# Both feed-forward fronts written as one: normalisation, router and shared feed-forward in one table-ordered program ahead of routing

## The chip, the cores and the metric

One Trainium2 core runs the whole kernel. The metric is the device time of one execution in microseconds, lower is better. A core has five instruction queues that matter here: PE (TensorE, matrix products), DVE (VectorE), ACT (ScalarE), POOL (GpSimd) and SP (SyncE, which only issues transfers). Each queue runs its own instructions in the order in which they are written; between queues there are only semaphores.

## The reference

The input is 4096 tokens of width 512. Three residual steps follow one another, and the change touches the first and the last.

```python
x = x + 0.5 * ffn(layernorm(x))        # first front and first expert stage
x = x + attention(layernorm(x))
x = x + 0.5 * ffn(layernorm(x))        # second front and second expert stage

def ffn(h):                            # E=32 experts, K=6, I=256, CAP=192
    logits = h @ gate_w.T
    scores = sqrt(softplus(logits))
    idx = top_k(scores + bias, K)                      # choice
    w = 1.5 * scores[idx] / sum(scores[idx])           # weights
    pos = running count of earlier choices of the same expert; valid = pos < CAP
    routed = sum over valid choices of w * down_e(silu(gate_e(h)) * up_e(h))
    shared = clip(silu(h @ sg.T) * (h @ su.T), -10, 10) @ sd.T
    return routed + shared
```

Products run on PE in fp32r after each operand has been split in a high part and a remainder (`hi`, `lo`), three products for one (`split_products`).

## The kernel before, in words

A feed-forward step has a front and an expert stage. The front must deliver `slots`, the table that says which token rows each expert gathers. The expert stage (`routed_experts`) then takes 32 experts in turn: POOL gathers 192 rows, PE computes, POOL adds the result to the output in memory.

The front works on G = 8 groups of 512 tokens. For a group, "norm and router" means: load `x`, statistics on DVE (L334), `h` on DVE (L347), 16 transposes on PE (L420), the high part on ACT (L295), the remainder on DVE (L354, L391), eight router products on PE (L428). "Shared work" of a group means gate and up (48 products of 512 columns) and down (24), with the silu on ACT, the product and the clip on DVE, the high part on ACT and the remainder.

Before, three programs stand one behind the other, each in a block of its own, so that all queues meet at its end. `setup` loads and splits constants and the shared weights. `dense_ffn` computes norm and router of all eight groups and the shared work of groups 0 to 4 (GA = 5): its loop body does the shared work of group g beside norm and router of group g+1, and groups 6 and 7 get norm and router alone behind the loop. In the first front POOL splits the attention weights there too (L282, L284). `route` computes the routing on DVE, with the shared work of groups 5 to 7 written between its steps (`inner`, L670 and L672; `add_residual`, L679), and remainders on POOL (L641). Its last part is the hot loop: for each of 32 tiles of 128 tokens DVE writes `hot_a` and `hot_b` (L777, L782), ACT scales `hot_a` by the tile number (L632), POOL scales it by the row number (L660), and PE adds eight small products to `r_ps_tab` (L874, L875).

Of the kernel before, what the change touches and what calls it, by code (L numbers as in the profile page):

```python
# [7 lines left out]
F32 = mybir.dt.float32  # L8
# [22 lines left out]
GA = 5  # L31
HT_OF = {5: 1, 6: 0, 7: 2}
# [32 lines left out]
NO_SLOT = 4000.0  # L65
SWIGLU_LIMIT = 10.0
# [22 lines left out]
def allocate_kept(nc, ctx):  # L89
    k = Kept()  # L90
    k.ffn_semaphores = []

    def sb(name, shape, dt):
        return ctx.enter_context(nc.sbuf_tensor(name, shape, dt))

    k.ident = sb("ident", [P, P], F32)
    k.causal_bf = sb("causal_bf", [P, P], BF16)
    k.ident_bf = sb("ident_bf", [P, P], BF16)
    k.upto_bf = sb("upto_bf", [P, P], BF16)
    k.ones_bf = sb("ones_bf", [P, P], BF16)  # L100
    k.ln_eps = sb("ln_eps", [P, 1], F32)
    k.rms_eps = sb("rms_eps", [P, 1], F32)
    k.shared_hi = sb("shared_hi", [P, WALL], F32R)
    k.shared_lo = sb("shared_lo", [P, WALL], F32R)
    k.router = sb("router", [P, KB, 3, E], F32R)
    k.wqkv_hi = sb("wqkv_hi", [P, KB, 6 * DH], F32R)
    k.wqkv_lo = sb("wqkv_lo", [P, KB, 6 * DH], F32R)
    k.wo_hi = sb("wo_hi", [P, H, D], F32R)
    k.wo_lo = sb("wo_lo", [P, H, D], F32R)
    return k  # L110


def setup(nc, a, k, htab, accs):

    with ExitStack() as ctx:
        sb = lambda name, shape, dt: ctx.enter_context(nc.sbuf_tensor(name, shape, dt))
        sem = lambda name: ctx.enter_context(nc.semaphore(name))
        raw_shared = sb("raw_shared", [P, WALL], F32)
        raw_router = sb("raw_router", [P, KB, E], F32)
        raw_causal = sb("raw_causal", [P, P], F32)  # L120
        raw_upto = sb("raw_upto", [P, P], F32)
        zeros = sb("zeros", [HALF, ROW], F32)
        no_weights = sb("no_weights", [P, KB, E], F32)
        zeroed, dumps, hi_ready = sem("setup_zeroed"), sem("setup_dumps"), sem("setup_hi")
        loaded = {name: sem(f"setup_loaded_{name}") for name in ("small", "shared", "shared_down")}
        with nc.Block() as block:

            @block.sync
            def _(sp):
                for name, dst, src in (("small", raw_router[:, :, :], a["router_w"]), ("small", k.ident[:, :], a["ident"]),  # L130
                                       ("small", raw_causal[:, :], a["causal"]), ("small", raw_upto[:, :], a["upto"]),
                                       ("shared", raw_shared[:, 0:WGU], a["w_shared"][:, 0:WGU]),
                                       ("shared_down", raw_shared[:, WGU:], a["w_shared"][:, WGU:])):
                    sp.dma_start(dst, src).then_inc(loaded[name], 16)

                sp.wait_ge(zeroed, 1)
                sp.dma_start(htab[DUMP:ROWS, :], zeros[:, :]).then_inc(dumps, 16)
                for acc in accs:
                    sp.dma_start(acc[DUMP:ROWS, :], zeros[:, 0:D]).then_inc(dumps, 16)
                sp.wait_ge(dumps, 16 * (1 + len(accs)))  # L140

            @block.gpsimd
            def _(pool):
                pool.memset(k.ones_bf[:, :], 1.0)
                pool.memset(no_weights[:, :, :], 0.0)
                pool.memset(k.ln_eps[:, :], LN_EPS)
                pool.memset(k.rms_eps[:, :], RMS_EPS)
                pool.memset(zeros[:, :], 0.0).then_inc(zeroed, 1)

            @block.scalar  # L150
            def _(act):
                act.wait_ge(zeroed, 1)
                act.activation(k.router[:, :, 2, :], no_weights[:, :, :], ACT.Copy)
                act.wait_ge(loaded["small"], 16 * 4)
                act.activation(k.router[:, :, 0, :], raw_router[:, :, :], ACT.Copy).then_inc(hi_ready, 1)
                act.activation(k.ident_bf[:, :], k.ident[:, :], ACT.Copy)
                act.activation(k.causal_bf[:, :], raw_causal[:, :], ACT.Copy)
                act.activation(k.upto_bf[:, :], raw_upto[:, :], ACT.Copy)
                act.wait_ge(loaded["shared"], 16)
                act.activation(k.shared_hi[:, 0:WGU], raw_shared[:, 0:WGU], ACT.Copy).then_inc(hi_ready, 1)  # L160
                act.wait_ge(loaded["shared_down"], 16)
                act.activation(k.shared_hi[:, WGU:], raw_shared[:, WGU:], ACT.Copy).then_inc(hi_ready, 1)

            @block.vector
            def _(dve):
                for n, (lo, raw, hi) in enumerate(((k.router[:, :, 1, :], raw_router[:, :, :], k.router[:, :, 0, :]),
                                                   (k.shared_lo[:, 0:WGU], raw_shared[:, 0:WGU], k.shared_hi[:, 0:WGU]),
                                                   (k.shared_lo[:, WGU:], raw_shared[:, WGU:], k.shared_hi[:, WGU:]))):
                    dve.wait_ge(hi_ready, n + 1)
                    dve.tensor_tensor(lo, raw, hi.bitcast(F32), ALU.subtract)  # L170


def dense_ffn(nc, a, k, n, src, acc, htab, logits, ht_hi, ht_lo):

    with ExitStack() as ctx:
# [10 lines left out]
        silu = [sb(f"d_silu{b}_", [P, GTOK], F32) for b in range(FB)]  # L189
        inter = [sb(f"d_inter{b}_", [P, GTOK], F32) for b in range(FB)]  # L190
        in_hi = [sb(f"d_in_hi{u}_", [P, FB, GTOK], F32R) for u in range(2)]
        in_lo = [sb(f"d_in_lo{u}_", [P, FB, GTOK], F32R) for u in range(2)]
        ps_t = [pb(f"d_ps_t{i}_") for i in range(2)]
        ps_gate = [pb(f"d_ps_gate{b}_") for b in range(FB)]
        ps_up = [pb(f"d_ps_up{b}_") for b in range(FB)]
        ps_down = [pb(f"d_ps_down{i}_") for i in range(2)]
        lg_t = sb("d_lg_t", [3 * E, GTOK], F32)

        d_bank = (ps_down[0], ps_down[1], ps_gate[0], ps_up[0])

        t_bank = lambda c, late: ps_gate[c - 2] if late and c >= 2 else ps_t[c % 2]
        lg_banks = lambda late: ps_up if late else ps_t
        x_loaded = [[sem(f"d_x_loaded{u}{m}_") for m in range(2)] for u in range(3)]
        h_stored = [sem(f"d_h_stored{u}_") for u in range(2)]
        y_stored = [sem(f"d_y_stored{u}_") for u in range(2)]
        stats_ready, std_ready, h_ready = sem("d_stats_ready"), sem("d_std_ready"), sem("d_h_ready")
# [1615 lines left out]
```

## Time and profile before

| | us |
|---|---|
| median of 3 runs | 1814.66 |
| lowest, highest | 1813.36, 1817.22 |
| the profiled execution's own time | 1805.24 |
| its span in the trace | 1803.5 |
| first front: slots written at | 281.3 |
| second front: first transposes, slots written | 1223.0, 1479.6 |

Times of the trace count from its first instruction. The profiled execution is 9.4 us below the median of the timed runs. PE is busy 85% of the span, DVE 65%, ACT 55%, POOL 43%; such shares are averages over stages with different limits, so the stages are read one by one. The granted PE clock is 1.00 at 2.4 GHz and 0.50 at 1.2 GHz.

### The profile page before, as it was taken

How to read it: one execution, taken by the hardware profiler on the slowest of the kernel's cores; microseconds unless marked ns; L12 is line 12 of the kernel's file. 1: busy time of each engine (PE TensorE's matmuls, PEld its weight loads, DVE VectorE, ACT ScalarE, POOL GpSimd, SP SyncE). 2: the span in 40 equal slices, each digit the busy share in tenths (PEclk: the TensorE clock that was granted, in tenths of full speed). 3: DMA queues.
4: the chain of work that ended last, by engine and by line, in shares of the span. 5: the costliest groups of instructions: out<-in, count | busy, mean ns of one | idle time of the engine just before them, and what ended most of it. 6: DMA issues, size and time to landing. Idle time of an engine off the chain costs nothing. (4 is left out here: it accounts for less than half of the span.)

```text
span 1803.5 us, 27507 instructions
## 1 busy us (share of the span) xinstructions
PE 1524.5 (85%) x8626; PEld 1256.3 (70%) x8628; DVE 1167.5 (65%) x2369; ACT 991.7 (55%) x2038; POOL 777.4 (43%) x677
## 2 busy tenths in 40 slices
PE   4997766999998289999999999878986759999994
PEld 3775555877777267887887887656765548787773
DVE  5666676777776156666666665645676577777773
ACT  3334144777776156666666666533333146777773
POOL 3000163556554376556557655310000263656653
PEclk9998887999999689999999999998997888999998
DMA  6444314999996211111111111014444316899994
GB/s 214 150 146 165 117 35 140 264 259 264 264 264 174 66 42 41 48 36 59 42 42 59 36 42 41 25 62 141 154 146 141 108 39 211 260 261 262 264 265 85
DMA packets 87196, 244.98 MB, mean 136 GB/s; under 512 B 17649, under 2 KB 18609, under 8 KB 78673
## 3 DMA queue, kind: packets, MB, share of 16 engines
q1 hardware_dynamic: 64592, 192.12, 31.2%
q0 software_dynamic: 22528, 51.92, 13.7%
q8 instruction: 40, 0.66, 0.1%
q14 instruction: 36, 0.29, 0.0%
HBM read 175.25 MB, written 68.76 MB: 135 GB/s over the span
## 5 line engine op out<-in xcount | busy, mean ns | idle before, releaser
L1077 DVE TENSOR_TENSOR e_w_lo<-e_raw,e_w_hi 128x1024 fp32r<-128x1024 f32 x192 | 233.9, 1219 | 109.8 <-ACT e_w_hi L1001 91.7
L1001 ACT ACTIVATE e_w_hi<-e_raw 128x1024 fp32r<-128x1024 f32 x192 | 202.5, 1056 | 29.6 <-PEq L570 17.0
L1582 POOL TENSOR_SCALAR t_prob<-t_prob,t_inv 128x128 f32<-128x128 f32 (+7 forms) x128 | 111.8, 873 | 221.0 <-DVE t_inv L1489 221.0
L1156 PE MATMUL e_ps_gate<-e_xt,e_w_hi 128*128 128x384 f32 x512 | 164.7, 384 | 28.8 <-DVE e_w_lo L1077 28.6
L953 POOL DMA_INDIRECT e_xg<-htab,e_gather_idx x128 | 138.5, 1082 | 63.1 <-issue 42.8
L1156 PE MATMUL e_ps_up<-e_xt,e_w_hi 128*128 128x384 f32 x512 | 151.9, 361 | 0.0
L964 POOL DMA_INDIRECT x_after_ffn<-e_y,e_add_idx x64 | 102.4, 1600 | 110.6 <-DMA x_after_ffn<-e_y,e_add_idx 87.9
L964 POOL DMA_INDIRECT out<-e_y,e_add_idx x64 | 102.3, 1598 | 110.4 <-DMA out<-e_y,e_add_idx 88.2
L1384 ACT ACTIVATE t_prob<-a_wide,t_neg_max,a_q_scale 128x128 f32<-128x128 f32 (+7 forms) x128 | 106.4, 831 | 53.3 <-DVE t_neg_max L1483 53.1
L1157 PE MATMUL e_ps_gate<-e_xt,e_w_lo 128*128 128x192 f32 x512 | 132.9, 260 | 0.0
L1157 PE MATMUL e_ps_up<-e_xt,e_w_lo 128*128 128x192 f32 x512 | 129.4, 253 | 0.0
L637 POOL MEMSET r_no_slots<- 128x96 bf16 x2 | 0.4, 180 | 295.8 <-POOLq L228 295.8
L1156 PEld LDWEIGHTS e_ps_gate<-e_xt,e_w_hi 128*128 128x128 f32 x512 | 101.0, 197 | 38.5 <-issue 21.9
L1494 DVE TENSOR_TENSOR t_pt<-a_bank,t_pt 128x512 fp32r<-128x512 f32 x144 | 96.3, 684 | 42.7 <-ACT t_pt L1391 41.9
L1391 ACT ACTIVATE t_pt<-a_bank 128x512 fp32r<-128x512 f32 x144 | 84.0, 596 | 69.2 <-PE a_bank L1659 68.9
L74 PE MATMUL e_ps_down<-e_w_hi,e_in_hi 128*96 128x512 f32 x256 | 101.1, 395 | 2.9 <-ACT e_y L1033 2.9
L1157 PEld LDWEIGHTS e_ps_gate<-e_xt,e_w_lo 128*128 128x128 f32 x512 | 102.4, 200 | 0.0
L76 PE MATMUL e_ps_down<-e_w_hi,e_in_lo 128*96 128x512 f32 x256 | 101.4, 396 | 0.0
L75 PE MATMUL e_ps_down<-e_w_lo,e_in_hi 128*96 128x512 f32 x256 | 100.2, 392 | 0.0
L1157 PEld LDWEIGHTS e_ps_up<-e_xt,e_w_lo 128*128 128x128 f32 x512 | 98.0, 191 | 0.0
L1481 DVE TENSOR_REDUCE t_top<-a_wide 128x1 f32<-128x128 f32 (+7 forms) x128 | 95.7, 748 | 1.6 <-PE a_wide L1651 1.6
L1156 PEld LDWEIGHTS e_ps_up<-e_xt,e_w_hi 128*128 128x128 f32 x512 | 96.5, 189 | 0.0
(318 smaller groups left out, 4644.7 us busy)
## 6 DMA issues: line engine op xcount, KB each, us to landing
e_raw<-in_w_experts SPq DMA_DIRECT2D x64, 1536.0 KB
htab<-d_h SPq DMA_DIRECT2D x16, 1024.0 KB, 4.2
d_x<-in_x SPq DMA_DIRECT2D x16, 512.0 KB, 5.0
q_x<-x_after_ffn SPq DMA_DIRECT2D x32, 256.0 KB, 3.2
t_res<-x_after_ffn SPq DMA_DIRECT2D x32, 256.0 KB, 2.6
x_after_attention<-t_res SPq DMA_DIRECT2D x32, 256.0 KB, 2.0
d_x<-x_after_attention SPq DMA_DIRECT2D x16, 512.0 KB, 5.4
x_after_ffn<-d_y SPq DMA_DIRECT2D x5, 1024.0 KB, 7.4
```

What stands on the lines that cost most here:

```text
L74: pe.matmul(out, wh, mh, start=first, stop=False)
L75: pe.matmul(out, wh, ml, start=False, stop=False)
L76: return pe.matmul(out, wl, mh, start=False, stop=last)
L953: pool.indirect_dma_start(xg[u][q][:, :], None, htab, bass.IndirectOffsetOnAxis(ap=gather_idx[u][:, q:q + 1], axis=0)).then_inc(gathered[u ...
L964: pool.indirect_dma_start(acc, bass.IndirectOffsetOnAxis(ap=add_idx[u][:, q:q + 1], axis=0), y[u][q][:, :], None, compute_op=ALU.add).then ...
L1001: act.activation(w_hi[u][:, cols], raw[u][:, cols], ACT.Copy).then_inc(hi_ready, 1)
L1077: dve.tensor_tensor(w_lo[u][:, cols], raw[u][:, cols], w_hi[u][:, cols].bitcast(F32), ALU.subtract).then_inc(lo_ready, 1)
L1156: pe.matmul(out, w[0][:, c, cols], xt[u][:, c, :, :], start=c == 0, stop=False)
L1157: got = pe.matmul(out[:, 0:CAP], w[1][:, c, cols], xt[u][:, c, 0, :], start=False, stop=c == KB - 1)
L1384: act.activation(prob[:, u, 0:width(i)], ps_s[i % 2][:, 0:width(i)], ACT.Exp, scale=q_scale[:, i // H % QSLOTS, i % H:i % H + 1], bias=neg ...
L1494: dve.tensor_tensor(pt[1][g % 3][:, :], bank("prob", T, c)[:, :], pt[0][g % 3][:, :].bitcast(F32), ALU.subtract).then_inc(p_lo, 1)
L1582: pool.tensor_scalar(prob[:, u, 0:width(i)], prob[:, u, 0:width(i)], inv[:, u:u + 1], 1.0, ALU.mult, ALU.mult).then_inc(p_ready, 1)
```

## The change

`setup`, `dense_ffn` and `route` become one function, `front`, in one block.

- Norm and router of the eight groups are the frame of every queue's program. `h` is now written by ACT (Identity with a scale and a shift), and the operands of six groups are kept (PLACES = 6) where there were three.
- The shared work is cut into 48 pieces (`piece`: gate, up or half of down, 12 products each). Tables (`PE_AT`, `DVE_AT`, ...) say behind which numbered spot of a queue's frame a piece is written. Up to spot 24 of PE (in group 6, behind its first two transposed chunks) there are 12 pieces, two to a group on the whole; at spot 24 there are 22; six are at each of 25 and 29; the last two at 30 and 31. No piece stands behind the start of routing.
- The clip and the remainder of all groups are on POOL; the hot loop has no POOL work and no tile-number product: ACT does the row number (L471), PE adds four products a tile, and the tile number comes from counts that DVE takes behind the loop (L664 to L672).
- The two halves of the logits are folded by PE with a constant matrix, where DVE added them.
- The residual input of the shared work is loaded again, a tile at a time (`xs`, six buffers), for all eight groups; it was loaded again for three.
- Constants and shared weights are loaded and split within the first front. The attention weights are loaded and split in the first expert stage: ten chunks of 128x512, one for each of experts 4 to 13, between a gather and a scatter on POOL.

```diff
-GA = 5
-HT_OF = {5: 1, 6: 0, 7: 2}
+PLACES = 6
+XS = 6
+PE_AT = (2, 4, 4, 4, 5, 5, 8, 9, 12, 13, 16, 17, 20, 21, 24, 24, 24, 24, 24, 24, 24, 24, 24, 24, 24, 24, 24, 24, 24,
+    24, 24, 24, 24, 24, 24, 24, 25, 25, 25, 25, 25, 25, 29, 29, 29, 29, 29, 29, 29, 29, 30, 30, 30, 31)
...
+        def at_spots(table, dense):
+            count = [0]
+
+            def spot():
+                for p in range(6 * G + 6):
+                    if table[p] == count[0] and piece(p)[0]:
+                        dense(*piece(p))
+                count[0] += 1
+            return spot
...
+                def dense(kind, g, b):
+                    if kind == "up":
+                        i = FB * g + b
+                        pool.wait_ge(mul_done, i + 1)
+                        pool.tensor_scalar(inter[i % 2][:, :], inter[i % 2][:, :], SWIGLU_LIMIT, -SWIGLU_LIMIT,
+                                           ALU.min, ALU.max).then_inc(clipped, 1)
+                        pool.wait_ge(ihi_ready, i + 1)
+                        pool.tensor_tensor(in_lo[g % 2][:, b, :], inter[i % 2][:, :], in_hi[g % 2][:, b, :].bitcast(F32),
+                                           ALU.subtract).then_inc(ilo_ready, 1)
...
+                for g in range(G):
+                    turn(g, 0)
+                    turn(g, 1)
+                    spot()
+                    if g:
+                        fold_logits(g - 1)
+                        spot()
+                    turn(g, 2)
+                    turn(g, 3)
+                    spot()
+                    router(g)
+                    spot()
+                fold_logits(G - 1)
+                spot()
...
+                for e in range(4, 4 + chunks):
+                    gather_next(e // 2, e % 2)
+                    split_chunk(e - 4)
+                    scatter(e // 2 - 1, e % 2)
```

What the program of a queue is at three places.

First, VectorE in the middle of the first front's routing, around the mask (L724 before, L599 after). Before:

```order
L714 SCALAR_TENSOR_TENSOR r_t_0<-r_seg,r_t_0 128x1024
L679 SCALAR_TENSOR_TENSOR r_xs_0<-r_ps_down,r_xs_0 128x512
L679 SCALAR_TENSOR_TENSOR r_xs_0<-r_ps_tab,r_xs_0 128x512
L718 TENSOR_TENSOR r_t_0<-r_t_0,r_per_tok 128x1024
L679 SCALAR_TENSOR_TENSOR r_xs_0<-r_ps_down,r_xs_0 128x512
L721 SCALAR_TENSOR_TENSOR r_t_0<-r_t_0 128x1024
L679 SCALAR_TENSOR_TENSOR r_xs_0<-r_ps_tab,r_xs_0 128x512
L724 TENSOR_TENSOR r_mask<-r_t_0 128x1024
L670 TENSOR_TENSOR r_inter<-r_silu,r_ps_up 128x512
L672 TENSOR_SCALAR r_inter<-r_inter 128x512
```

and after:

```order
L590 SCALAR_TENSOR_TENSOR r_t_0_74<-r_seg,r_t_0_73 128x1024
L593 TENSOR_TENSOR r_t_0_75<-r_t_0_74,r_per_tok 128x1024
L596 SCALAR_TENSOR_TENSOR r_t_0_74<-r_t_0_75,r_t_0_73 128x1024
L599 TENSOR_TENSOR r_mask_79<-r_t_0_74,r_t_0_72 128x1024
L606 COPY r_t_0_72<-d_ps_lg 128x32x16
L606 COPY r_t_0_72<-d_ps_fold 128x32x16
```

The residuals and the product of shared work (L679, L670) have gone from between the steps; the routing steps stand directly behind one another.

Second, ScalarE in group 6 of the first front, after the change (L399 is the high part of a transposed chunk, L413 the silu, L418 the high part of a shared product, L387 the normalisation of the next group):

```order
L379 ACT_TABLE_LOAD
L379 ACTIVATE d_std_0<-d_mv_0,ln_eps 128x4
L399 ACTIVATE ht_hi_0_59<-d_ps_t_0 128x512 x2
L418 ACTIVATE d_in_hi_0<-d_inter_0 128x512
L413 ACT_TABLE_LOAD
L413 ACTIVATE d_silu_0<-d_ps_gate 128x512
L418 ACTIVATE d_in_hi_0<-d_inter_0 128x512
L413 ACTIVATE d_silu_0<-d_ps_gate 128x512
...
L399 ACTIVATE ht_hi_0_59<-d_ps_t_0 128x512 x2
L387 ACTIVATE d_h_0_70<-d_x_0_68,d_shift_0,d_rstd_0 128x512 x4
```

The pair of L413 and L418 repeats through group 5 before the last two chunks of group 6 (L399) are taken, so the shared work of groups 2 to 5 stands ahead of the routers of groups 6 and 7; before, groups 6 and 7 had their routers behind group 4.

Third, GpSimd in the first expert stage, before:

```order
L973 COPY e_gather_idx_0<-slots 96x2 x2
L953 DMA e_xg_0<-htab,e_gather_idx_0 96x544 x10
L964 DMA x_after_ffn<-e_y_0,e_add_idx_0 4192x512 x2
L953 DMA e_xg_0<-htab,e_gather_idx_0 96x544 x2
L964 DMA x_after_ffn<-e_y_0,e_add_idx_0 4192x512 x2
```

and after:

```order
L898 DMA e_xg_0<-htab,e_gather_idx_0 96x544 x10
L909 DMA x_after_ffn<-e_y_0,e_add_idx_0 4192x512 x2
L898 DMA e_xg_0<-htab,e_gather_idx_0 96x544 x2
L909 DMA x_after_ffn<-e_y_0,e_add_idx_0 4192x512 x2
L898 DMA e_xg_0<-htab,e_gather_idx_0 96x544 x2
L915 CAST wqkv_hi<-d_xs_0 128x512
L917 TENSOR_TENSOR wqkv_lo<-d_xs_0,wqkv_hi 128x512
```

A cast (L915) and a subtraction (L917) of one chunk of attention weights now stand between a gather (L898) and a scatter (L909).

## Rows read from the trace of the kernel before

**Rows 1.** The page: span.
```profile
span 1803.5 us, 27507 instructions
```

**Rows 2.** Busy time by stretch, with PE clock, DMA share and GB/s.
```profile
core 0: us, PE busy (x) PEld busy (x) DVE busy (x) ACT busy (x) POOL busy (x), PEclk, DMA share, GB/s
...
52.00:74.00 22.00, 21.45 (x104) 16.81 (x103) 14.13 (x29) 8.09 (x12) 0.00 (x0) 1.00 0.43 144
142.00:166.30 24.30, 13.30 (x65) 9.47 (x63) 15.72 (x38) 7.66 (x14) 0.00 (x0) 0.78 0.35 130
166.30:281.30 115.00, 81.76 (x489) 63.92 (x490) 82.54 (x165) 38.60 (x55) 40.18 (x41) 0.87 0.28 92
1223.00:1362.10 139.10, 124.11 (x584) 96.82 (x584) 87.68 (x181) 50.49 (x78) 0.00 (x0) 0.96 0.42 144
1362.10:1479.60 117.50, 83.18 (x489) 65.13 (x490) 82.84 (x165) 38.50 (x55) 40.61 (x41) 0.87 0.27 90
340.00:400.00 60.00, 54.97 (x344) 47.23 (x342) 44.90 (x81) 44.34 (x80) 35.43 (x26) 1.00 0.90 260
```

**Rows 3.** Timeline, first front: issue of x, h, transposes, first router product.
```profile
14.56 1.97 SPq L233 DMA_DIRECT2D d_x<-in_x  x4
...
22.02 1.92 DVE L347 TENSOR_SCALAR d_h<-d_x,d_mv,d_rstd 128x512 f32<-128x512 f32 x4
...
23.99 1.97 PE L420 MATMUL d_ps_t<-ident,d_h 128*128 128x128 f32 x8 [23.99 <-DVE d_h L347]
...
29.89 0.74 PE L428 MATMUL d_ps_t<-ht_hi,router 128*96 128x512 f32 x1 [1.41 <-DVE ht_lo L354]
```

**Rows 4.** Timeline, PE: first and last of 24 gate and up products; transposes.
```profile
197.27 0.40 PE L74 MATMUL r_ps_gate<-ht_hi,shared_hi 128*128 128x512 f32 x1
...
202.64 0.40 PE L76 MATMUL r_ps_up<-ht_hi,shared_lo 128*128 128x512 f32 x1
...
148.03 1.94 PE L420 MATMUL d_ps_t<-ident,d_h 128*128 128x128 f32 x8 [3.80 <-DVE logits L359]
...
156.07 1.09 PE L420 MATMUL d_ps_t<-ident,d_h 128*128 128x128 f32 x8
```

**Rows 5.** Waits in the first routing, 166.3 to 281.3 us: total, times, longest.
```profile
DVE r_inter L670 <- ACT r_silu L612: 10.2, 2, 6.6
...
PE r_ps_gate L74 <- POOL r_in_lo L641: 6.9, 1, 6.9
...
DVE r_hot_a L777 <- PE r_ps_tab L875: 6.8, 1, 6.8
...
DVE r_t L685 <- ACT r_t L605: 3.5, 1, 3.5
```

**Rows 6.** Groups by line, VectorE, same stretch: count | busy, mean ns.
```profile
L670 DVE TENSOR_TENSOR r_inter<-r_silu,r_ps_up 128x512 f32<-128x512 f32 x4 | 2.7, 684 | 10.2 <-ACT r_silu L612 10.2
L679 DVE SCALAR_TENSOR_TENSOR r_xs<-r_ps_tab,r_xs 128x512 f32<-128x512 f32 x4 | 2.7, 684 | 0.5 <-PE r_ps_tab L76 0.5
```

**Rows 7.** Timeline, VectorE: two tiles of the hot loop.
```profile
248.10 0.42 DVE L782 TENSOR_TENSOR r_hot_b<-r_slot_b,r_iota_b 128x512 bf16<-128x512 bf16 x1
...
248.71 0.42 DVE L782 TENSOR_TENSOR r_hot_b<-r_slot_b,r_iota_b 128x512 bf16<-128x512 bf16 x1
```

**Rows 8.** Groups by line: scaling a hot tile on GpSimd and ScalarE.
```profile
L660 POOL TENSOR_SCALAR r_part_a<-r_hot_a,r_part_id 128x384 bf16<-128x384 bf16 x64 | 56.7, 903 | 13.3 <-DVE r_hot_a L777 12.9
...
L632 ACT ACTIVATE r_tile_a<-r_hot_a,r_tile_id 128x384 bf16<-128x384 bf16 x64 | 39.3, 615 | 32.7 <-DVE r_hot_a L777 32.7
```

**Rows 9.** Timeline: VectorE's normalise beside GpSimd's split.
```profile
33.36 3.48 POOL L284 TENSOR_TENSOR wqkv_lo<-d_y,wqkv_hi 128x1536 fp32r<-128x1536 f32 x1
...
36.16 6.68 DVE L347 TENSOR_SCALAR d_h<-d_x,d_mv,d_rstd 128x512 f32<-128x512 f32 x4
```

**Rows 10.** Waits in the first expert stage, 300 to 560 us.
```profile
POOL x_after_ffn L964 <- DMA x_after_ffn<-e_y,e_add_idx: 74.9, 26, 4.3
...
PE e_ps_gate L1156 <- DVE e_w_lo L1077: 14.1, 23, 0.8
```

More of the change, by code:

```diff
@@ L105, in allocate_kept @@
     k.router = sb("router", [P, KB, 3, E], F32R)
[L106 to L109, printed above, removed]
-    return k
[L113 to L170, printed above, removed]
@@ new lines, in allocate_kept, with piece, place_of_group, staged_buffers @@
+    return k
+def piece(p):
+    g, r = divmod(p, 6)
+    kind = ("gate", "up", "down")[r % 3]
+    there = g > 0 if kind == "down" else g < G
+    return (kind, g - 1 if kind == "down" else g, r // 3) if there else (None, g, 0)
+def place_of_group(g):
+    return g % PLACES
+def staged_buffers(nc, places, name, u, n):
+    part = KB * GTOK * 4
+    at = (nc.sbuf_base + 31) // 32 * 32
+    places.enter_context(nc.sbuf_tensor(f"{name}{u}_{n}", [P, 2 * KB * GTOK], F32))
+    hi = nc.alloc_sbuf_tensor_at(f"ht_hi{u}_{n}", [P, KB, GTOK], F32R, offset=at)
+    lo = nc.alloc_sbuf_tensor_at(f"ht_lo{u}_{n}", [P, KB, GTOK], F32R, offset=at + part)
+    return at, hi, lo
@@ L178, in dense_ffn, with front @@
+def front(nc, a, k, n, src, acc, accs, htab, slots, staged, raw, xs, w_loaded, y_stored):
     with ExitStack() as ctx:
@@ L201, in dense_ffn @@
[L201 to L206, printed above, removed]
-        t_ready, t_hi, t_lo = sem("d_t_ready"), sem("d_t_hi"), sem("d_t_lo")
@@ L604, in _ @@
+                act.wait_ge(lg_taken, G)
+                for u in range(2):
+                    act.wait_ge(h_stored[u], 16 * (G // 2))
+                act.activation(t2[:, :, :], logits[:, :, :], ACT.Abs)
                 act.drain()
@@ new lines, in router @@
+                def router(g):
+                    pe.wait_ge(t_lo, 4 * g + 4)
+                    if g:
+                        pe.wait_ge(lg_out, g)
+                    elif n == 0:
+                        pe.wait_ge(setup_lo, 1)
+                    at = place_of_group(g)
+                    for c in range(KB):
+                        for part, ht in enumerate((ht_hi, ht_lo)):
+                            got = pe.matmul(ps_lg[0:3 * E, :], k.router[:, c, :, :].rearrange("p s e -> p (s e)"),
+                                            ht[at][:, c, :], start=(c == 0 and part == 0),
+                                            stop=(c == KB - 1 and part == 1))
+                    got.then_inc(lg_ready, 1)
```

1028 lines of the change are left out of this document (495 added, 533 removed).

## The prediction

> **What bounds the kernel now.** I read the windows first, stage by stage, because the change leaves attention alone and touches the expert stages only by ten small pieces of work. The span is 1803.5 us [rows 1]; the two fronts end at 281.3 and 1479.6. A front has two halves. Up to the last logits PE is the bound: a loop body of 22.0 us holds 21.45 us of PE work at clock 1.00, with ACT busy 8.09 and DVE 14.13 [rows 2]. Behind the loop the last two groups get norm and router alone, and 24.3 us pass with PE busy 13.3 and its clock at 0.78 [rows 2]. The second half, the routing, takes 115.0 and 117.5 us, and there VectorE's chain is the bound (busy 82.5), because the queue holds shared work too and waits for it: 10.2 us in two waits for a silu, 6.8 for the hot tables while PE finishes the last down products, themselves 6.9 late on a remainder of GpSimd [rows 2, 5].
>
> So time between first transposes and slots is 281.3 - 24.0 = 257.3 and 1479.6 - 1223.0 = 256.6 us [rows 2, 3].
>
> **The change, part by part.** I rebuild both halves of a front; T is the first transposes, L the last logits.
>
> *T to L.* All shared work is now here, so this half gets longer. Twelve products of a piece cost half of 24; the first and the last of 24 start 5.37 us apart over 23 steps, so 0.2335 each and 2.80 a piece [rows 4]. 47 of the 48 pieces stand ahead of the last logits: 131.7. Sixteen pairs of transposed chunks at 0.95 (8 transposes last 1.09, and the next start before that end) [rows 4]: 15.2. Eight routers of eight products, 0.2335 each: 14.9. Eight folds, smaller than a pair of chunks, 0.5 each: 4.0. Together 165.8 of PE work. What PE cannot cover: the first group's chain from transposes to router, 5.9 us with 1.9 of work in it [rows 3], so 4; the last two chunks of groups 6 and 7, which have no piece between them and the gate that needs them, 1.8 each; the last logits' way through VectorE, 0.5. That is 173.9. For stalls that I cannot see I add 3: 177. Bounds: 0 and, by the rival below, some 20.
>
> Why should PE run through? In the interleaved groups 1 to 5 it has 2 pieces, 4 chunks, router and fold, 9.8 us. ScalarE has four more instructions a group than in the old body (h). At 0.6 each (a scaling of 384 columns takes 0.615 [rows 8]) that is 8.09 + 2.4 = 10.5 in the old body, but a group now has about half of the old body's silus and splits, so near 9.0 of 9.8. That is close. VectorE loses h and clip and gets 7 to 8. Followed queue by queue, each chunk's high part and remainder end under the piece that stands behind it, with about 1 us to spare; where ScalarE changes its table for silu and for square root, the margin is smallest. GpSimd's clip and remainder: 3.48 us for 1536 columns and 0.903 for 384 are both 2.3 ns a column [rows 8, 9], so 1.2 each for 512; product, clip, high part and remainder take about 4, and two or three pieces (5.6 to 8.4) stand between an up and the down that needs it. Hidden. If the cover were gone (one piece, 2.8), it would cost 1.2 for each of eight groups. Loads: five more groups' inputs, 5 MB a front, at a DMA share of 0.42 and 0.28 [rows 2]; hidden. On SP a tile's store waits for its residual ahead of the store of the last h; that h is read by nobody until routing.
>
> *T itself.* In the first front x was issued at 14.56 and transposed at 23.99, 9.4 later [rows 3], behind the setup block. Now x is issued third in SP's queue, near 1.7. With 9.4 plus a little for h on ScalarE (4 at about 0.55 against 1.92 for four [rows 3]) T comes at 11.5. But gate of group 0 waits for the shared weights behind 3.8 MB of transfers, split by near 23 us, about 3.5 later than PE would be there. So L = 11.5 + 177 + 3.5 = 192. The second front keeps T = 1223.5 and gives L = 1400.5, where it was 1362.1.
>
> *L to slots.* From 115: VectorE is busy 82.5. Shared work leaves it: six products and twelve residuals at 0.684 [rows 6] and six clips at some 0.4, 14.7. The hot loop: with GpSimd running a tile takes 0.90 (its own instruction, 0.903), at a moment without it 0.61, two hot tables apart [rows 7, 8]; ScalarE's scaling takes 0.615, so 0.62 is the new pace and 28 tiles give 8.0 back. Adding the logits' halves and small steps: 1.8. New: tile numbers, two passes over 1024 columns and two reductions, up to 1.2 each, 4.5 (bounds 2.5 and 6). Busy 62.5. Waits that stay: exponent 3.5 [rows 5], square root with its table 2.5, the counting products 2, last products and transposes 2.2, drains 2.5: 12.7. Sum 75 (bounds 70 and 82).
>
> Slots: 192 + 75 = 267, 14.3 earlier; 1400.5 + 75 = 1475.5, 4.1 earlier. Fronts: -18.4.
>
> *Expert stage of the first step.* Ten chunks on GpSimd, 1.2 for the subtraction and about 0.6 for the cast. GpSimd waits there for the landing of the last addition, 74.9 us in 26 waits, 2.9 each [rows 10], and the chunk stands ahead of just that wait: hidden. Their 2.6 MB come at a DMA share of 0.90 and 260 GB/s [rows 2]: 10 us if nothing is free; six of ten are issued at the stage's start, when the weights of experts 0 and 1 are there and those of expert 2 are not yet asked for, so 4 chunks, 1 MB, 4 us at full price, less half for the tenth that is free. 2 us. And VectorE beside GpSimd: four normalisations of h took 6.68 beside a split and 1.92 alone, 4.8 more for 3.5 of GpSimd's work [rows 3, 9]. PE waits for the weights' remainder of VectorE already, 23 times, 0.6 each [rows 10], so a delay there reaches it. I take 0.2 a chunk, 2 us; bounds 0 and, if VectorE loses all the 1.8 us of a chunk and PE all of VectorE's, 18. Stage: +4.
>
> The Trainium skill (SBUF — State Buffer, "Who interferes with whom") says that a VectorE instruction with two inputs in SBUF contends with a GpSimd instruction that reads SBUF, and that whoever is first holds the port for its whole instruction. The weights' remainder is such an instruction, and the trace bears the rule out in kind [rows 9]; by it a chunk can cost the whole 1.8 us, ten of them 18, which is the third rival below.
>
> **Sum.** -14.3 - 4.1 + 4 = -14.4. Against the profiled execution's span, 1803.5 gives 1789.1; against the median of the runs, which lies 9.4 above that execution's time, 1814.7 gives 1800. A measurement tells this kernel from itself to about 0.2%, 3.6 us.
>
> **Rivals.**
> Margins hold better (faster still): no stalls where I allow 3 a front and nothing in the expert stage: -14.4 - 6 - 4 = -24, 1790. For it: the old loop ran at 21.45 of 22.0. Against: the new interleaving is tighter.
> The interleaved groups run at the pace of their chain, not of PE (slower). The two late groups show that chain bare: 24.3 us for two, 12.2 each [rows 2]. If half of a piece more stands uncovered, 13.5 against my 9.8, for five groups in two fronts: +37, less the 6 allowed: 1800 + 31 = 1831. The transposes after a wait of 3.80 us took 1.94 against 1.09 [rows 4], the lower of PE's two clock levels, so such gaps also slow what follows. It decides from 11.9 us a group, where 6 + 14.4 are eaten. Against it: pieces stand where those groups had nothing.
> GpSimd's splits block VectorE in the expert stage: +18 for +4, so -0.4: 1814, no change. Against it: GpSimd there mostly issues gathers and has 2.9 of slack.
> That nothing is gained because the hidden work comes back is half true already: 16.8 us of shared work for each of three groups leaves a routing that covered it, and L moves 26 to 38 later. That is in the sum.
>
> **Numbers.** Forecast 0.48 (own range 1793 to 1808), faster still 0.20, chain pace 0.22, blocking 0.10. The predicted time is 1800. From 1783 to 1819 takes in the first, second and fourth and the mild end of the third. Faster 0.68, same 0.11 (blocking, and the middle of the chain's case), slower 0.21.
>
> **What would show it.** T near 11.5; last logits near 192 and 1400; routing near 75 with VectorE hardly waiting; hot pace 0.62; PE busy over 0.93 of T to L at clock 1.00; an expert pace near 9.0 us also for experts 4 to 13. The prediction is wrong if interleaved groups take 12 us or more, if the hot loop stays at 0.9 (then something other than GpSimd slowed it, +9 a front), or if the first expert stage grows by more than 10.

## The result: 2.25% slower, and the profile after

The changed kernel takes 1855.42 us (median of 4 runs, 1853.50 to 1858.60), the kernel before 1814.45 (4 runs, 1813.36 to 1817.22): ratio 1.0225, 95% interval 1.0207 to 1.0244. I had said 1800, between 1783 and 1819. So 41 us are lost where 14 were to be won.

First the page of the profiled execution, its span and the slices that the loss stands in (40 equal ones, a digit is a tenth).

```profile
span 1853.1 us, 26194 instructions
...
PE   6999448767799648999999999996999547999985
...
DMA  7735117765899621111101111115646105999994
```

The span is 49.6 longer [rows 1]. From the seventh to the eleventh slice, the first expert stage, PE stands at 6 to 8 tenths and DMA falls to 5; in the second expert stage, at the right end, nothing of the kind is seen. Busy time by stretch says the same, and it says how the fronts did:

```profile
15.00:199.60 184.60, 177.17 (x821) 142.22 (x822) 75.89 (x150) 77.49 (x123) 30.50 (x32) 0.98 0.58 190
199.60:273.40 73.80, 26.24 (x157) 18.95 (x157) 63.51 (x146) 27.44 (x39) 4.08 (x2) 0.55 0.08 19
273.00:400.00 127.00, 93.61 (x517) 83.52 (x516) 73.56 (x128) 70.17 (x119) 66.47 (x51) 0.83 0.70 203
400.00:500.00 100.00, 70.55 (x387) 62.42 (x388) 49.61 (x87) 52.41 (x91) 54.84 (x39) 0.88 0.63 172
500.00:600.00 100.00, 90.70 (x576) 79.10 (x575) 72.84 (x131) 70.95 (x129) 60.19 (x46) 1.00 0.92 259
1276.30:1300.00 23.70, 21.63 (x98) 17.16 (x99) 11.07 (x25) 14.44 (x25) 1.89 (x2) 0.80 0.69 244
1276.30:1456.70 180.40, 173.86 (x821) 140.26 (x822) 72.38 (x148) 74.28 (x118) 30.52 (x32) 0.96 0.56 189
1456.70:1530.10 73.40, 26.27 (x157) 18.96 (x157) 63.47 (x146) 27.44 (x39) 4.08 (x2) 0.54 0.08 19
```

The first row is T to L of the first front, the second its routing; the last two are those of the second front. PE is busy 177.2 of 184.6 us, and routing takes 73.8 and 73.4 where it took 115.0 and 117.5 [rows 2]. But from 400 to 500 PE is busy 70.6 of 100 and the DMA share is 0.63; it was 0.90 with PE at 0.92 in a stretch of that stage before [rows 2].

I cut the span of each execution at six moments: slots of the first front written (S1), first and last of the experts' scaled outputs in that stage (`e_y`), first maximum of attention, first transposes of the second front (T2), its slots (S2). Worked out from the traces by the starts of these instructions, one trace a kernel, in us:

```
kernel               S1    to first  all of its  to attention  to T2   to S2   to end   span
                           output    rounds
before              281.0    30.4      274.2        63.7       573.7   256.3   324.2   1803.5
changed             273.2    31.7      333.6        63.0       574.8   253.6   323.2   1853.1
semaphore           274.5    34.1      281.5        65.2       574.8   253.8   323.4   1807.3
before, bare drain  285.6    31.6      356.2        64.3       574.1   259.0   325.8   1896.6
doubled remainder   271.9    34.2      301.0        64.6       576.3   253.9   323.3   1825.2
hot on GpSimd       282.7    34.4      283.7        64.9       576.4   263.2   323.2   1828.5
half chunks         271.4    30.7      281.6        65.2       575.2   255.0   325.9   1805.0
wait for landing    271.9    34.6      334.3        65.0       574.7   254.9   323.5   1858.9
late loads          273.4    30.4      282.5        64.4       574.8   253.7   324.0   1803.2
chunk first         271.8    34.3      316.7        63.7       574.9   253.8   325.9   1841.1
double loads        269.7    30.2      282.8        65.2       573.9   254.8   324.0   1800.6
eighth loads        273.7    28.9      281.2        64.1       574.7   255.2   323.3   1801.1
loads in routing    271.5    29.0      281.9        64.5       573.4   253.7   324.6   1798.6
half splits         273.8    29.0      278.0        63.8       575.0   255.1   323.5   1798.2
```

Of the 49.6, the rounds of the first expert stage hold 59.4 (333.6 for 274.2); both fronts together win 10.5. All of the loss is in one stage. What waits there:

```profile
PE e_ps_t L1100 <- DMA e_xg<-htab,e_gather_idx: 67.1, 17, 10.5
...
POOL x_after_ffn L909 <- DMA x_after_ffn<-e_y,e_add_idx: 48.3, 14, 5.9
...
POOL wqkv_lo L917 <- issue: 30.8, 6, 6.6
...
POOL wo_lo L917 <- issue: 19.2, 4, 5.3
```

PE waits 67.1 us for gathered tokens (273 to 600 us); before, the same wait was 17.6 in all (281 to 600 us). GpSimd, which issues the gathers, stands still 50 us in 10 waits ahead of a chunk's remainder, and no releaser is named ("issue"). Its timeline shows one round of an expert (start, length, line, instruction, idle time before it):

```profile
349.53 1.48 POOL L898 DMA_INDIRECT e_xg<-htab,e_gather_idx  x1 [0.30 <-issue]
...
353.33 0.62 POOL L915 CAST wqkv_hi<-d_xs 128x512 fp32r<-128x512 f32 x1
359.01 1.26 POOL L917 TENSOR_TENSOR wqkv_lo<-d_xs,wqkv_hi 128x512 fp32r<-128x512 f32 x1 [5.07 <-issue]
360.44 1.48 POOL L909 DMA_INDIRECT x_after_ffn<-e_y,e_add_idx  x1 [0.17 <-issue]
...
364.52 1.47 POOL L898 DMA_INDIRECT e_xg<-htab,e_gather_idx  x1 [0.30 <-issue]
```

Two gathers, the chunk's high part (0.62), 5.07 us of nothing, its remainder (1.26), two additions; the next gathers come 15.0 after the last. PE's row of the same moment names the event at which the gap ends, the landing of the gathers (DMA e_xg):

```profile
358.85 1.54 PE L1100 MATMUL e_ps_t<-ident,e_xg 96*128 96x96 f32 x8 [3.69 <-DMA e_xg<-htab,e_gather_idx]
```

The gathers have landed by 358.85, and GpSimd's remainder starts at 359.01. One round earlier it is 343.95 and 344.12. The trace has the landing events themselves: in nine of the ten rounds the remainder starts 0.30 us after the last of the round's gathers has landed, in the first 0.89. Between the high part and the remainder the new code has a drain (`pool.drain()`), written there so that the remainder starts only when the high part is complete, and that is the suspect.

### The profile page after: what moved, and what is told of

It is laid out like the page before. It is cut to its first block and busy times, and to the rows that moved or that the text cites. A ratio compares the mean times of both kernels' runs of the same rounds, so it can differ in the third digit from the quotient of the medians.

```text
span 1853.1 us, 26194 instructions
## 1 busy us (share of the span) xinstructions
PE 1530.9 (83%) x8434; PEld 1272.3 (69%) x8436; DVE 1099.7 (59%) x2274; ACT 1029.0 (56%) x2096; POOL 780.2 (42%) x679
## 3 DMA queue, kind: packets, MB, share of 16 engines
q0 software_dynamic: 22528, 51.92, 13.6%
## 5 line engine op out<-in xcount | busy, mean ns | idle before, releaser
L1111 PE MATMUL e_ps_gate<-e_xt,e_w_hi 128*128 128x384 f32 x512 | 178.7, 408 | 21.4 <-DVE e_w_lo L1032 20.5
L898 POOL DMA_INDIRECT e_xg<-htab,e_gather_idx x128 | 145.3, 1135 | 66.0 <-issue 39.0
L909 POOL DMA_INDIRECT out<-e_y,e_add_idx x64 | 103.3, 1614 | 109.1 <-DMA out<-e_y,e_add_idx 87.2
L909 POOL DMA_INDIRECT x_after_ffn<-e_y,e_add_idx x64 | 104.1, 1627 | 87.8 <-DMA x_after_ffn<-e_y,e_add_idx 65.2
L1112 PE MATMUL e_ps_gate<-e_xt,e_w_lo 128*128 128x192 f32 x512 | 139.2, 272 | 0.0
L353 POOL TENSOR_SCALAR d_inter<-d_inter 128x512 f32<-128x512 f32 x32 | 19.6, 614 | 277.5 <-DVE d_inter L518 277.5
L1100 PE MATMUL e_ps_t<-ident,e_xg 96*128 96x96 f32 x512 | 61.6, 269 | 84.6 <-DMA e_xg<-htab,e_gather_idx 83.8
L1111 PEld LDWEIGHTS e_ps_gate<-e_xt,e_w_hi 128*128 128x128 f32 x512 | 109.4, 214 | 28.3 <-issue 17.5
L1100 PEld LDWEIGHTS e_ps_t<-ident,e_xg 96*128 96x128 f32 x512 | 52.9, 154 | 102.5 <-issue 78.4
L1112 PEld LDWEIGHTS e_ps_gate<-e_xt,e_w_lo 128*128 128x128 f32 x512 | 110.7, 216 | 0.0
```

Source lines behind the costliest of these rows:

```text
L898: pool.indirect_dma_start(xg[u][q][:, :], None, htab, bass.IndirectOffsetOnAxis(ap=gather_idx[u][:, q:q + 1], axis=0)).then_inc(gathered[u ...
L909: pool.indirect_dma_start(acc, bass.IndirectOffsetOnAxis(ap=add_idx[u][:, q:q + 1], axis=0), y[u][q][:, :], None, compute_op=ALU.add).then ...
L1100: got = pe.transpose(ps_t[c][:, at:at + HALF], xg[u][q][:, (2 * c + b) * P:(2 * c + b + 1) * P], k.ident[0:HALF, 0:HALF])
L1111: pe.matmul(out, w[0][:, c, cols], xt[u][:, c, :, :], start=c == 0, stop=False)
L1112: got = pe.matmul(out[:, 0:CAP], w[1][:, c, cols], xt[u][:, c, 0, :], start=False, stop=c == KB - 1)
```

## The experiments

Theory D: a drain on GpSimd waits for the gathers that it issued just before. Rivals: P, VectorE holds the remainder back by the shared port; L, the chunks' loads take the transfers' time. The kernels of one batch share their runs of the kernel before (medians 1819.4, 1817.4 and 1816.7 us in the three batches), so kernels of different batches are compared by their ratios.

**1. A semaphore for the drain.**

```diff
-                    pool.tensor_copy(hi, xs[c % XS][:, :])
-                    pool.drain()
+                    pool.tensor_copy(hi, xs[c % XS][:, :]).then_inc(att_hi, 1)
+                    pool.wait_ge(att_hi, c + 1)
```

> The changed kernel, in which GpSimd waits on a semaphore of its own high-part instruction where it drained between the high part and the remainder of a chunk. Theory D (the drain also waits until the gathers that GpSimd issued just ahead of it have landed, 4.1 to 6.6 us a chunk, and so stretches ten experts from 9.1 to 14.6 us): the gap between the two instructions falls below 0.5 us, the pace returns to about 9.1 to 9.3, and the time falls by 50 to 60, to 1795 to 1806. Rival P (the remainder is held back by VectorE's instructions on the same memory): the gap and the time stay, 1850 or more. Rival L (the chunks' loads steal from the weights' and the gathers' transfers): the gap goes or stays, but the pace remains above 12 us, 1835 or more.

1808.50 us, ratio 0.9948 (0.9929 to 0.9967): one line turns 2.25% slower into 0.5% faster. P and L fall as causes of the gap: the remainder is still there, still beside VectorE, and so are the loads. One round, on GpSimd:

```profile
360.96 2.35 POOL L910 DMA_INDIRECT x_after_ffn<-e_y,e_add_idx  x1 [0.16 <-DVE e_gather_idx L1046]
363.61 1.44 POOL L910 DMA_INDIRECT x_after_ffn<-e_y,e_add_idx  x1 [0.30 <-issue]
365.35 1.30 POOL L899 DMA_INDIRECT e_xg<-htab,e_gather_idx  x1 [0.30 <-issue]
366.96 0.96 POOL L899 DMA_INDIRECT e_xg<-htab,e_gather_idx  x1 [0.31 <-issue]
367.91 1.54 POOL L916 CAST wqkv_hi<-d_xs 128x512 fp32r<-128x512 f32 x1
369.54 1.29 POOL L918 TENSOR_TENSOR wqkv_lo<-d_xs,wqkv_hi 128x512 fp32r<-128x512 f32 x1
```

The gap is 0.1. Seven of the ten rounds last 10.0, not the 9.1 that I expected: more of that in 3, 5, 9 and 10.

**2. The drain alone, in the kernel before.** After the gathers of experts 4 to 13 of the first stage:

```diff
+                for e in range(4, 4 + alone):
+                    gather_next(e // 2, e % 2)
+                    pool.drain()
+                    scatter(e // 2 - 1, e % 2)
```

> The kernel before, with nothing added but a bare drain of GpSimd behind the gathers of experts 4 to 13 of the first expert stage; no chunks, the old fronts. Theory D: GpSimd's round for an expert becomes two gather issues, the wait for their landing and two addition issues, 14.6 less the 2.2 of a chunk's two instructions, so 12.4 against 9.1: +33, 1840 to 1855. Rivals P and L: nothing is there for the drain to wait for, 1815 as before.

1900.40 us, ratio 1.0456 (1.0428 to 1.0483). Ten bare drains cost twice what the change lost. In kind D is right and the rivals are out: there is no chunk here. In size I was wrong. Two rounds, the first from among the ten, the second from behind them:

```profile
369.92 1.47 POOL L964 DMA_INDIRECT x_after_ffn<-e_y,e_add_idx  x1 [5.37 <-issue]
...
374.43 1.47 POOL L953 DMA_INDIRECT e_xg<-htab,e_gather_idx  x1 [0.30 <-issue]
...
383.19 1.47 POOL L964 DMA_INDIRECT x_after_ffn<-e_y,e_add_idx  x1 [5.70 <-issue]
...
499.02 2.43 POOL L964 DMA_INDIRECT x_after_ffn<-e_y,e_add_idx  x1 [0.30 <-issue]
501.76 1.46 POOL L953 DMA_INDIRECT e_xg<-htab,e_gather_idx  x1 [0.30 <-issue]
...
509.51 1.47 POOL L964 DMA_INDIRECT x_after_ffn<-e_y,e_add_idx  x1 [5.04 <-DMA x_after_ffn<-e_y,e_add_idx]
```

The ten take 13.2 each where I worked out 12.4; in nine of them the addition starts 1.17 us after the gathers' landing. But the rounds behind them, with no drain, stay at 11.8 until the last experts, where the kernel before has about 9.1: now GpSimd waits 4 to 5 us for the landing of additions, and PE for gathers that were issued late. In the changed kernel the rounds fell back to about 9.1 soon after the last chunk. Why a late round stays late here isn't settled; no further run was made for it.

**3. The remainder twice.**

```diff
-                    pool.tensor_tensor(lo, ..., ALU.subtract).then_inc(att_split, 1)
+                    pool.tensor_tensor(lo, ..., ALU.subtract).then_inc(att_hi, 1)
+                    pool.wait_ge(att_hi, 2 * c + 2)
+                    pool.tensor_tensor(lo, ..., ALU.subtract).then_inc(att_split, 1)
```

> The changed kernel with the semaphore, and the remainder of each of the ten chunks computed twice in a row (1.27 us more of GpSimd a chunk, same output). If GpSimd's wait for the last additions (2.9 us a round before) hides a chunk: within 2 us of the kernel with the semaphore. If GpSimd's instruction blocks VectorE's remainders for its length and PE waits for it, as the third rival of the prediction has it: +13.

1828.58 us, ratio 1.0056 (1.0033 to 1.0079), 1.1% over the first run. The rounds are 19.5 longer, 1.95 for each of ten. Neither theory had that: the added instruction takes longer than the 1.27 it takes alone. One round:

```profile
349.28 2.22 POOL L918 TENSOR_TENSOR wqkv_lo<-d_xs,wqkv_hi 128x512 fp32r<-128x512 f32 x1
351.58 2.13 POOL L920 TENSOR_TENSOR wqkv_lo<-d_xs,wqkv_hi 128x512 fp32r<-128x512 f32 x1
```

Here both last over 2.1, where 1.28 is the bare length; the twenty of the ten rounds take 33.3 in all, the ten of experiment 1 12.9. PE's largest wait in these rounds (319 to 436 us) is for the gathers:

```profile
PE e_ps_t L1103 <- DMA e_xg<-htab,e_gather_idx: 18.4, 6, 4.3
```

What follows: with a second remainder GpSimd has no slack left, waits for nothing in eight of the ten rounds, and issues the gathers late.

**4. The hot tables scaled on GpSimd again.**

```diff
-                    act.activation(part_a[t % HOTS][...], hot_a[t % HOTS][...], ACT.Copy, scale=part_id[:, :])
+                    pool.tensor_scalar(part_a[t % HOTS][...], hot_a[t % HOTS][...], part_id[:, :], 1.0,
+                                       ALU.mult, ALU.mult)
```

> The changed kernel with the semaphore, and the scaling of the hot tables put back on GpSimd. If GpSimd's part of the hot loop set the pace of 0.90 a tile, by its own 0.903 or by holding VectorE: pace 0.9 for 0.62, 28 tiles, +8 a front, +16 in all. If the pace came from something else that the change removed: no difference.

1826.02 us, ratio 1.0039 (1.0020 to 1.0058), so 17.5 over the first run for 16 expected. First VectorE in the changed kernel, then here, then GpSimd here:

```profile
249.41 0.41 DVE L651 TENSOR_TENSOR r_hot_b<-r_slot_b,r_iota_b 128x512 bf16<-128x512 bf16 x1
...
250.01 0.41 DVE L651 TENSOR_TENSOR r_hot_b<-r_slot_b,r_iota_b 128x512 bf16<-128x512 bf16 x1
```

```profile
255.83 0.72 DVE L653 TENSOR_TENSOR r_hot_b<-r_slot_b,r_iota_b 128x512 bf16<-128x512 bf16 x1
...
256.73 0.72 DVE L653 TENSOR_TENSOR r_hot_b<-r_slot_b,r_iota_b 128x512 bf16<-128x512 bf16 x1
...
253.53 9.10 POOL L375 TENSOR_SCALAR r_part_a<-r_hot_a,r_part_id 128x384 bf16<-128x384 bf16 x10
```

A tile takes 0.60 and here 0.91, the same as GpSimd's 9.10 for ten; hot_b itself grows from 0.41 to 0.72. The first front's slots come 8.2 later, and the second front from T to its slots is 9.4 longer. So GpSimd's part did set the pace of the old hot loop. The Trainium skill (SBUF — State Buffer, "Who interferes with whom") says that VectorE and GpSimd share a pair of ports and that whoever holds it shuts the other out; 0.72 for 0.41 on VectorE here, and 2.2 for 1.28 on GpSimd in experiment 3, agree with it in kind.

**5 and 6. Half chunks; waiting for the landing itself.** The fifth cuts the ten chunks into twenty of 256 columns. The sixth keeps the semaphore and adds the very wait that the drain is thought to be:

```diff
                     pool.wait_ge(att_hi, c + 1)
+                    pool.wait_ge(gathered[e % 2], 32 * (e // 2 + 2))
```

> The kernel with the semaphore, its ten chunks of 512 columns cut into twenty of 256, one for each of experts 4 to 23. With ten chunks GpSimd waits only 0.16 us in most rounds of 10.0 us, so it sets the pace there and 0.9 us of each round comes on top of 9.1. If a round costs only what exceeds the slack (2.9 us before), a half chunk of about 1.5 us with its overhead fits: pace 9.1 to 9.4, 5 to 9 us faster than with whole chunks. If every chunk costs its share whatever its size, because it holds VectorE or the memory: twenty halves cost as much as ten wholes, no difference.

> The kernel with the semaphore, and between a chunk's high part and its remainder one more wait, on the semaphore of the two gathers just issued, so until they have landed; no drain. If the drain costs what it costs because it lasts until the gathers have landed, this has the changed kernel's pace of 14.6 and its time, +41 to +52 against the semaphore alone. If the drain has a cost of its own (a queue emptied, a restart), this is at least 15 us faster than the changed kernel.

Half chunks: 1805.74 us, 0.9931 (0.9910 to 0.9951); the interval overlaps that of the first run. Its rounds take 281.6 in all, those of the ten whole chunks 281.5: as the second theory has it, a chunk costs its share whatever its size. But the cost has changed its place: from 325 to 500 us PE waits 5.0 for VectorE's remainder of the weights, where it is 19.8 with whole chunks, and 13.6 for gathers, where it is 1.6.

Waiting for the landing: 1856.49 us, 1.0215 (1.0171 to 1.0259), the changed kernel's 1.0225 again, and its rounds take 334.3 against 333.6. GpSimd:

```profile
384.19 0.87 POOL L916 CAST wqkv_hi<-d_xs 128x512 fp32r<-128x512 f32 x1
390.64 1.27 POOL L919 TENSOR_TENSOR wqkv_lo<-d_xs,wqkv_hi 128x512 fp32r<-128x512 f32 x1 [5.59 <-DMA e_xg<-htab,e_gather_idx]
```

The gap of 5.59 is now put down to the gathers' landing by name. A semaphore on the landing and the drain cost the same, as far as the runs tell: the drain has next to no cost of its own beside it. By the landing events the remainder starts 0.15 after the landing here, and 0.30 with the drain.

**7. Late loads.** No chunk is loaded ahead of the first gathers; each is loaded two rounds before its use.

> The kernel with the semaphore, its chunks' loads issued two rounds before their use, so none ahead of the first gathers. With six loads there, the first gathered tokens reach TensorE 10.2 us after the slots, 8.0 before, and the first addition comes 38.1 after the slots, 34.0 before. If the six loads (1.5 MB, 6 us of transfer) delay the gathers: 2 to 4 us faster. If the delay is the table load for silu (1.28 us) and the clock: no difference.

1805.04 us, 0.9939 (0.9915 to 0.9964). By the runs alone that is not told from the first kernel; by the trace the place is clear. The first gathered tokens reach PE, with six loads ahead and with none:

```profile
284.60 1.54 PE L1101 MATMUL e_ps_t<-ident,e_xg 96*128 96x96 f32 x8 [10.17 <-DMA e_xg<-htab,e_gather_idx]
```

```profile
280.78 1.54 PE L1100 MATMUL e_ps_t<-ident,e_xg 96*128 96x96 f32 x8 [7.43 <-DMA e_xg<-htab,e_gather_idx]
```

10.1 and 7.4 us after the slots (274.5 and 273.4), and the first output comes after 30.4 instead of 34.1. By this pair of traces the six loads cost 3.7. Four other traces with six whole loads have 34.2 to 34.6, but that of the changed kernel, with the same loads, has 31.7, and why isn't known. The rounds are 282.5, hardly changed.

**8. The chunk ahead of the gathers.** The changed kernel with its drain; the additions are under way when it drains.

```diff
-                    gather_next(e // 2, e % 2)
                     split_chunk(e - 4)
+                    gather_next(e // 2, e % 2)
```

> The changed kernel with its drain, each chunk ahead of the round's gathers instead of behind them, so that at the drain the additions of the round before are under way, not gathers. If the drain waits for every transfer that GpSimd has issued: it lasts until those additions have landed, some 5 us, and the pace is 12.5 to 14.5, +35 or more against the semaphore. If it waits for gathers alone: the pace is about 10 and the time that of the semaphore.

1844.24 us, 1.0165 (1.0124 to 1.0205), some 39 over the semaphore. The ten gaps are 5.2, 2.1, 2.5, 1.4, 1.4, 7.1, 5.9, 6.9, 5.7 and 5.4. One of the short and one of the long:

```profile
374.02 1.59 POOL L917 TENSOR_TENSOR wqkv_lo<-d_xs,wqkv_hi 128x512 fp32r<-128x512 f32 x1 [1.36 <-DVE e_gather_idx L1045]
...
382.65 1.11 POOL L915 CAST wqkv_hi<-d_xs 128x512 fp32r<-128x512 f32 x1
390.87 1.47 POOL L917 TENSOR_TENSOR wqkv_lo<-d_xs,wqkv_hi 128x512 fp32r<-128x512 f32 x1 [7.11 <-issue]
```

The drain is not tied to gathers alone: by the landing events the remainder starts 0.30 after the last addition has landed in nine of the ten rounds, and 0.81 in the first. That also explains the short gaps. In those four rounds the second addition lands 4.2 to 4.5 us after its start, in the six others 7.1 to 9.7, and the drain ends with it each time. Why the landing is quick in some rounds and slow in others isn't known.

**9 and 10. What sets the 10.0?** Two theories are left for the rounds with a chunk: M, transfers; G, GpSimd's own work. The ninth loads each chunk twice, the tenth only 64 of its 512 columns (the kernel then leaves out seven eighths of attention's weights; GpSimd's arithmetic is whole).

> The kernel with the semaphore and late loads, each chunk's 256 KB loaded a second time into a buffer that is free (same arithmetic, same output). Theory M (the expert stage is bound by transfers: 264 GB/s at a DMA share of 0.92 before, so 0.26 MB more is 1.0 us more in a round, 9.0 to 10.0, and twenty halves cost what ten wholes cost): rounds with a chunk go from 10.0 to 11.0, +8 to +10. Theory G (GpSimd is full in these rounds, so its 1.9 us for a chunk set the pace): no difference.

> The kernel with the semaphore and late loads, of each chunk only 64 of 512 columns are loaded (the rest is what the buffer held, so attention has wrong weights); GpSimd's arithmetic stays whole. Theory M: rounds of 9.1 to 9.3 in place of 10.0, 6 to 8 us faster than with whole loads. Theory G: rounds of 10.0, no difference. If both limits lie at 10.0, this shows no gain and the halved arithmetic of the fourth run does.

1804.37 us (0.9933, 0.9910 to 0.9956) and 1804.20 us (0.9928, 0.9901 to 0.9954), rounds 282.8 and 281.2 where one whole load a chunk gave 282.5: an eighth of the bytes and twice the bytes make no difference. Busy time of the two, 330 to 400 us:

```profile
330.00:400.00 70.00, 60.22 (x354) 51.67 (x353) 53.83 (x85) 46.23 (x85) 60.11 (x43) 0.95 0.97 290
```

```profile
330.00:400.00 70.00, 62.02 (x369) 54.68 (x369) 53.59 (x85) 47.23 (x88) 60.35 (x42) 0.94 0.89 247
```

The DMA share is 0.97 and 290 GB/s in one, 0.89 and 247 in the other, at one pace. M falls: more was moved in the same time. GpSimd's full round in experiment 1 adds up without it: additions 2.35 and 1.44, gathers 1.30 and 0.96, chunk 1.54 and 1.29, gaps 0.16 + 0.30 x 3 + 0.08: 10.0.

That GpSimd doesn't wait is not yet that PE waits for GpSimd, and there is a theory that I left out here, though it is the third rival of the prediction: V, a chunk on GpSimd holds VectorE, and PE waits for VectorE. Two rows of VectorE in experiment 1, the second of them in the kernel before, and PE's only wait in the ten rounds of experiment 1 (321 to 421 us):

```profile
377.49 1.55 DVE L1033 TENSOR_TENSOR e_w_lo<-e_raw,e_w_hi 128x1024 fp32r<-128x1024 f32 x1 [1.63 <-ACT e_w_hi L959]
...
380.01 0.89 DVE L1046 COPY e_gather_idx<-slots 96x2 uint32 x1
```

```profile
378.64 0.16 DVE L1090 COPY e_gather_idx<-slots 96x2 uint32 x1
```

```profile
PE e_ps_gate L1112 <- DVE e_w_lo L1033: 13.8, 9, 1.8
```

A remainder of the weights that takes 1.22 before takes 1.55 beside the chunk's high part, and a copy of 0.16 takes 0.89 and ends where the chunk's remainder ends (380.87): 1.06 a round. PE waits up to 1.8 a round for VectorE, and for no gather; in the same ten rounds before (324 to 416 us) it waits 4.5 for VectorE and 2.0 for gathers. Over the stage VectorE's instructions last 9.5 longer in all, each taken against its median before, and the rounds are 7.3 longer. So by the traces whole chunks cost their time as V has it, and the doubled remainder of experiment 3 as G has it. No run separates the two: the bytes of 9 and 10 leave GpSimd's and VectorE's rows alike.

**11 and 12. A version for use.** The first six chunks are loaded in the first routing (DMA share 0.08, second row of the windows above), four late; the twelfth also cuts each chunk's arithmetic into halves.

> The kernel with the semaphore, the first six chunks loaded during the first routing, where the DMA share is 0.08, the other four late in the expert stage. Theory M: six rounds without extra traffic, 4 to 6 us faster than with late loads alone. Theory G: rounds with a chunk stay at 10.0, 0 to 1 us faster.

> The same, with each chunk's arithmetic in two halves of 256 columns in rounds 4 to 23, the loads as in the run before. Theory M: as the run before, within 1.5 us. Theory G, or both limits at 10.0: rounds of 9.0 to 9.3 throughout, another 3 to 5 us faster, which makes about 0.989 of the kernel before.

1802.72 us, 0.9919 (0.9891 to 0.9948), and 1799.24 us, 0.9899 (0.9870 to 0.9928): the last is 1.0% faster than the kernel before and, by the two ratios, 3.2% faster than the changed one. Half a chunk in it:

```profile
350.67 1.11 POOL L922 CAST wqkv_hi<-d_xs 128x256 fp32r<-128x256 f32 x1
351.87 0.74 POOL L924 TENSOR_TENSOR wqkv_lo<-d_xs,wqkv_hi 128x256 fp32r<-128x256 f32 x1
```

The two instructions take 1.11 and 0.74. The rounds where GpSimd doesn't wait last about 9.1, the twenty 9.4 on the mean, and all rounds 278.0 for 274.2 before. The halves help here by 3.9 in the rounds, and by nothing in experiment 5 with its fourteen small loads between the weights'. PE's waits show where the difference lies: from 325 to 500 us it waits 8.2 for gathers here, 13.6 there and 2.7 in the kernel before. What makes those gathers late isn't known, and the two intervals of 11 and 12 overlap.

## Why the prediction was wrong

**The step that failed** is the first of the expert stage: "GpSimd waits there for the landing of the last addition, 74.9 us in 26 waits, 2.9 each, and the chunk stands ahead of just that wait: hidden." I priced the chunk's two instructions, and not the drain that stands between them. It holds GpSimd until the gathers have landed, 4.1 to 6.6 us. The additions of the round, and all that GpSimd does behind them, had to wait for that landing, and the next gathers went out 15 us after the last; PE waited for their tokens. Forecast for the stage +4, measured +60.0 from S1 to attention, of which +47.5 go with the drain (experiment 1) and +12.5 stay. What misled me: the same pair with the same drain stood in the kernel before, in the first front, and cost nothing there:

```profile
31.76 1.45 POOL L282 CAST wqkv_hi<-d_y 128x1536 fp32r<-128x1536 f32 x1
```

Its remainder starts at 33.36 [rows 9], 0.15 behind. GpSimd had no gather under way there.

**The same step without the drain** was too small as well. The 2.9 of slack has room for a chunk alone (0.62 + 1.29 and gaps, 2.0), but in the full rounds the high part takes 1.54, and the first addition 2.35 where it took 1.81 on the mean of the same ten rounds before (1.46 to 2.42). Of the 12.5, 3.7 lie ahead of the first output, 7.3 in the rounds and the rest behind them. The 7.3 stand against the term for VectorE beside GpSimd, which I took at 2 between 0 and 18: mis-sized, and by the traces the third rival's mechanism at under half its bound (9 and 10). Experiment 3 shows that GpSimd had no room for more, and 9 and 10 that it is not transfers. The transfers' term, 2 us, was 3.7 by experiment 7, all at the stage's start, and 1.3 by the changed kernel's own trace.

**T to L** was right in kind, and the chain-pace rival did not come: logits of the interleaved groups follow each other in 10.2 to 10.8 us.

```profile
45.09 0.29 DVE L507 TENSOR_SCALAR d_logits<-d_ps_fold 128x128 f32<-128x128 f32 x1 [1.13 <-PE d_ps_fold L728]
55.26 0.29 DVE L507 TENSOR_SCALAR d_logits<-d_ps_fold 128x128 f32<-128x128 f32 x1 [1.12 <-PE d_ps_fold L728]
76.18 0.29 DVE L507 TENSOR_SCALAR d_logits<-d_ps_fold 128x128 f32<-128x128 f32 x1 [0.93 <-PE d_ps_fold L728]
```

The step took 180.4 in the second front for my 177, and 184.6 for 180.5 in the first (177 and the wait for shared weights). PE's work was mis-sized, 173.9 for 165.8: its clock is at 0.80 over the first 23.7 us (sixth row of the windows), between its two levels, 1.2 and 2.4 GHz, and each of eight folds takes 1.05, not 0.5. Waits took 6.5 of my 11.2. T came at 15.0 for 11.5: ScalarE waited for the setup's small loads until 7.5, VectorE behind it, and four scalings of h took 2.9.

**L to slots** was right: 73.8 and 73.4 for 75, a hot tile in 0.60 for 0.62, and experiment 4 confirms the reason.

**Fronts in sum.** S1 is 7.8 earlier than in the profiled execution of before, and T2 to S2 2.7 shorter, for 14.3 and 4.1. But that execution was itself below its median by 9.4. In experiment 2, whose fronts are those of before, the same two measures are 285.6 and 259.0; against these the changed fronts win 12.4 and 5.4, 17.8 for my 18.4. With +60.0 for the stage (against the kernel before), +0.7 for attention and 2.6 less in the last stage (against experiment 2) that makes +40.3, and the runs say 41. It is an account from single traces; against the kernel before alone the fronts win 10.5.

With the semaphore 0.9948 was reached for a forecast of 0.9921, some 9 us of the 14: the right direction, with the stage's other terms still too small.

## What to carry to other kernels

Before work is put into a stage on an engine that issues transfers, list every instruction of it with its waits and drains, and ask of each what is under way on that engine at that moment: the same drain is free in one stage and 5 us in the next. Order an engine's own two instructions by a semaphore on the first, and the transfers stay out of it. And a slack of 2.9 us hides 2.9 us of work as it will run there, not its length from a quiet stretch: a round's rows, added up, tell when the engine is full. Then look at what the bounding engine waits for: an engine without idle time need not be the one that is waited for.

## What the runs showed of the hardware

- A drain on GpSimd lasted as long as a wait on its gathers' landing (gaps of 4.1 to 6.6 us, rounds 333.6 against 334.3), and 0.15 with none under way. With additions under way the gap was 1.4 to 7.1. In 18 of these 20 rounds (changed kernel, experiment 8) the next instruction started 0.30 after the last landing.
- GpSimd's high part of 512 columns took 0.62 to 2.14 us and its remainder 1.26 to 2.24. VectorE's remainder of the weights took 1.55 for 1.22 beside the one, and a copy of 96x2 took 0.89 for 0.16 beside the other.
- A late round can stay late: 11.8 us a round behind the ten drains, with no drain in it.
- The DMA share of 0.90 to 0.92 in the expert stage was no limit in rounds of 10.0: 0.97 and 290 GB/s ran at the same pace. For rounds of 9.1 no run shows it.
